# Sums of weight blocks moved to GpSimd with new orders on every engine, and zero products round TensorE's first products

## The reference, cut to what matters

```python
gate = lora_add(einsum('bnh,fh->bnf', x, W_gate), x, A_gate, B_gate)   # F = 1376, H = 512
up   = lora_add(einsum('bnh,fh->bnf', x, W_up), x, A_up, B_up)
act  = silu(gate) * up
down = lora_add(einsum('bnf,hf->bnh', act, W_down), act, A_down, B_down)
# lora_add(base, inp, A, B) = base + 0.5 * (inp @ A[idx].T) @ B[idx].T
x = x + down
x = x + einsum('bct,bcd->bdt', x, weights[condition])
```

## Time and profile before

| | |
|---|---|
| median of 3 runs | 457.99 us (457.64 to 458.76) |
| the profiled execution | 457.48 us |
| its span | 455.6 us |
| TensorE busy | 437.4 us (96%), 2465 matmuls |
| VectorE busy | 335.0 us (74%), 621 instructions |
| ScalarE busy | 213.3 us (47%), 396 |
| GpSimd busy | 168.2 us (37%), 156 |

### The profile page before, as it was taken

How to read it: one execution, slowest core, us unless ns; L and a number is a source line. 1 busy time by engine, 2 the same in 40 slices (tenths; PEclk the granted TensorE clock), 3 DMA queues, 4 the chain that set the end, 5 groups by cost and what they waited for, 6 DMA issues and landing times.

```text
span 455.6 us, 7248 instructions
## 1 busy us (share of the span) xinstructions
PE 437.4 (96%) x2465; PEld 393.9 (86%) x2465; DVE 335.0 (74%) x621; ACT 213.3 (47%) x396; POOL 168.2 (37%) x156
## 2 busy tenths in 40 slices
PE   5999999977999999999999999988999999999997
PEld 4978988865898888888888888988999999999996
DVE  6778698876876866967867857976766676676665
ACT  6664334365436335444444444925434545433441
POOL 3612120120311211111111551675566676665630
PEclk9999999999899999999999999999999999999999
DMA  8965663325667467466475589787556666555631
GB/s 268 378 221 150 182 181 108 104 81 147 167 170 210 109 163 193 112 199 157 112 205 148 141 260 337 196 201 201 170 173 192 205 199 202 176 175 175 201 104 46
DMA packets 99699, 81.12 MB, mean 178 GB/s; under 512 B 50928, under 2 KB 83056, under 8 KB 99664
## 3 DMA queue, kind: packets, MB, share of 16 engines
q1 hardware_dynamic: 88368, 47.27, 37.1%
q0 software_dynamic: 11008, 33.30, 24.0%
q10 hardware_dynamic: 288, 0.10, 0.1%
HBM read 65.18 MB, written 15.47 MB: 177 GB/s over the span
## 4 chain that ended last, share of the span: by engine, by line
PE 86%; DVE 7%; DMA 2%; ACT 2%; issue 1%; SPq 1%; DVEq 0%; ACTq 0%
PE bank L1300 24%; PE bank L1146 9%; PE bank L1147 9%; PE bank L1148 8%; PE bank L1191 8%; PE bank L1192 8%; PE bank L1193 8%; PE bank L1214 4%; PE bank L1213 4%; PE bank L1330 2%; DVE wd L763 2%; DMA actT_raw<-actT_dram 2%; PE bank L1310 1%; DVE b_gu L767 1%; PE bank L1315 1%
## 5 line engine op out<-in xcount | busy, mean ns | idle before, releaser
L441 POOL DMA_INDIRECT b_raw<-in_b_rows,rows x48 | 50.8, 1059 | 199.3 <-DVE b_gu L767 198.7
L1300 PE MATMUL bank<-wd,actT_hi 128*128 128x288 f32 x648 | 112.0, 295 | 3.1 <-DVE actT_lo L763 1.9
L1300 PEld LDWEIGHTS bank<-wd,actT_hi 128*128 128x128 f32 x648 | 95.5, 188 | 4.7 <-issue 3.5
L441 POOL DMA_INDIRECT a_dn_raw<-in_a_dn_rows,rows x64 | 75.5, 1180 | 19.5 <-issue 19.5
L767 DVE SCALAR_TENSOR_TENSOR b_gu<-b_raw,low_rows,b_gu 128x1024 fp32r<-128x1024 f32 (+1 forms) x48 | 55.6, 1159 | 30.6 <-ACT b_gu L500 30.6
L1300 PE MATMUL bank<-wd,actT_lo 128*128 128x288 f32 (+1 forms) x324 | 69.4, 296 | 0.0
L1300 PEld LDWEIGHTS bank<-wd,actT_lo 128*128 128x128 f32 (+1 forms) x324 | 51.9, 188 | 0.0
L500 ACT ACTIVATE b_gu<-b_raw 128x1024 fp32r<-128x1024 f32 (+1 forms) x48 | 46.2, 963 | 12.2 <-DMA b_raw<-in_b_rows,rows 10.7
L585 ACT ACTIVATE act<-bank 128x512 f32<-128x512 f32 (+1 forms) x48 | 26.2, 547 | 44.1 <-PE bank L1214 43.9
L763 DVE TENSOR_TENSOR actT_lo<-actT_raw,actT_hi 128x1280 fp32r<-128x1280 f32 (+1 forms) x32 | 27.0, 885 | 15.5 <-ACT actT_hi L500 14.6
L872 DVE TENSOR_TENSOR act<-act,bank 128x512 f32<-128x512 f32 (+1 forms) x48 | 29.9, 622 | 8.1 <-PE bank L1214 7.3
(11 more groups left out here) (177 smaller groups left out, 993.8 us busy)
## 6 DMA issues: line engine op xcount, KB each, us to landing
actT_raw<-actT_dram SPq DMA_DIRECT2D x16, 640.0 KB
actT_dram<-staging SPq DMA_DIRECT2D x64, 128.0 KB, 2.8
x_sb<-in_x SPq DMA_DIRECT2D x16, 256.0 KB, 2.9
xT_raw<-in_xT SPq DMA_DIRECT2D x15, 256.0 KB, 3.0
out<-out_sb SPq DMA_DIRECT2D x15, 256.0 KB, 2.0
a_raw<-in_a_gu_rows SPq DMA_DIRECT2D x56, 64.0 KB, 2.4
actT_dram<-staging SPq DMA_DIRECT2D x32, 88.0 KB, 3.1
wd_raw<-in_w_down SPq DMA_DIRECT2D x10, 256.0 KB, 7.1
```

Source lines behind the costliest of these rows:

```text
L441: return pool.indirect_dma_start(dst, None, src, bass.IndirectOffsetOnAxis(ap=rows[:, tile, col:col + 1], axis=0))
L1300: last = pe.matmul(ps_down[e][half][:, 0:HALF], a[e][0:n, c, :], wd[0:n, c, part, at:at + HALF], start=(c == 0 and i == 0), stop=(c == NC ...
```

## The change

The eight sum operations go from VectorE's queue to GpSimd's, where they stand between the gathers of pair 1. The forms are split in the order t2, t1, t4, t3, the first six of the eight parts in pair 1, t3 in pair 2. TensorE multiplies zeros (a 128x128 block by itself, into an unused bank) 34 times before its first product and 8 times after the first slice of it, as soon as VectorE has zeroed `mix_hi` and `mix_lo`. In the fast pairs the waits for the adapter halves move behind the first product of their pair of matrices. In the last pair five, not four, wd chunks are split early and at other places; the last two gatings go behind the preparation of tile 1, whose down products no longer wait for them, and the load of tile 2 goes ahead of the last spill.

The diff, cut to its core; lines with # say where a piece stands, and indentation is taken off:

```diff
+ZEROS_FIRST, ZEROS_BETWEEN = 34, 8
-SPLITS = [(f, m) for f in ("t2", "t3", "t1", "t4") for m in MATRICES]
+SPLITS = [(f, m) for f in ("t2", "t1", "t4", "t3") for m in MATRICES]
# SP, after the last pair
 load_x(0, 0)
+load_actT(2, 0)
 load_x(1, 1)
 spill(PAIRS - 1, 2)
-load_actT(2, 0)
 load_actT(3, 1)
# GpSimd: pair 1 is pair_with_sums(1); the other pairs are as before
+def sum_weights(f, i):
+    if f == "t3":
+        pool.wait_ge(w_ready, GU_PIECES)
+    elif f != "t1":
+        pool.wait_ge(weights_summed, 4 if f == "t2" else 6)
...
+    nc.gpsimd.tensor_tensor(block_raw(f, m), block_raw(a, m), block_raw(b, m), ALU.subtract)\
+        .then_inc(weights_summed, 1)
+def pair_with_sums(pr):
+    gather_b(pr, 1, 0)
+    gather_b(pr, 1, 1)
+    sum_weights("t3", 0)
+    sum_weights("t3", 1)
+    sum_weights("t1", 0)
+    sum_weights("t1", 1)
+    gather_b(pr, 2, 0)
+    sum_weights("t2", 0)
+    sum_weights("t2", 1)
+    gather_b(pr, 2, 1)
+    sum_weights("t4", 0)
+    sum_weights("t4", 1)
+    gather_b(pr + 1, 0, 0)
+    gather_b(pr + 1, 0, 1)
# ScalarE: split_forms, split_s
-    elif f == "t1":
-        sc.wait_ge(w_ready, GU_PIECES + i)
-        sc.wait_ge(weights_summed, 8)
     elif f == "t3":
         sc.wait_ge(xT_used[1], PLAIN)
-    else:
+    elif m == "up":
+        sc.wait_ge(w_ready, GU_PIECES + i - (1 if f == "t1" else 0))
+        sc.wait_ge(weights_summed, 8)
+    elif f == "t4":
         sc.wait_ge(w_ready, GU_PIECES + i)
...
-        sc.wait_ge(w_ready, GU_PIECES + 4)
+        sc.wait_ge(w_ready, GU_PIECES + 8)
# ScalarE: plain_pair
-split_forms(0, 2)
 silu(pr, 2)
 split_b(pr, 2, 0)
+split_forms(0, 2)
 split_x(pr + 1, 0)
 silu(pr, 3)
 split_b(pr, 2, 1)
+split_forms(2, 3)
 split_x(pr + 1, 1)
+split_forms(3, 6)
# ScalarE: fast_pair
-    split_forms(2, 4)
 copy_p1(pr)
 split_b(pr, 1, 0)
 silu(pr, 1)
 if first:
+    split_forms(6, 8)
     split_s(pr)
-    split_forms(4, 6)
     silu(pr, 2)
+    split_b(pr, 1, 1)
     copy_p7(pr)
-    split_forms(6, 8)
-    split_b(pr, 1, 1)
...
 if not last:
     split_x(pr + 1, 0)
+else:
+    split_down(0, 3)
...
-    split_down(0, 4)
+    split_down(3, 5)
# VectorE: plain_pair
-sum_weights("t3")
 gating(pr, 0)
 split_b(pr, 1, 0)
-sum_weights("t1")
 gating(pr, 1)
 split_b(pr, 1, 1)
-sum_weights("t2")
 split_a(pr + 1, 0)
 split_a(pr + 1, 1)
-split_forms(0, 2)
 gating(pr, 2)
 split_b(pr, 2, 0)
+split_forms(0, 2)
 split_x(pr + 1, 0)
 gating(pr, 3)
-sum_weights("t4")
 split_b(pr, 2, 1)
+split_forms(2, 3)
 split_x(pr + 1, 1)
 sum_x(pr + 1)
+split_forms(3, 6)
# VectorE: fast_pair
 split_b(pr, 0, 1)
-if first:
-    split_forms(2, 4)
 split_b(pr, 1, 0)
 if first:
+    split_forms(6, 8)
     split_s(pr)
 gating(pr, 1)
-if first:
-    split_forms(4, 6)
-else:
-    split_b(pr, 1, 1)
+split_b(pr, 1, 1)
 gate(pr, 2)
+if last:
+    split_down(0, 1)
 add_u3(pr, 0)
...
+    split_down(1, 2)
 add_u7(pr, 0)
+if last:
+    split_down(2, 3)
 add_u7(pr, 1)
# ScalarE, after the pairs
-split_down(4, NC)
-silu(PAIRS - 1, 4)
+split_down(5, NC)
 split_a_dn(1, 1)
-silu(PAIRS - 1, 5)
 sc.wait_ge(s_used, FAST)
 split_actT(1, 1)
+silu(PAIRS - 1, 4)
+silu(PAIRS - 1, 5)
...
+split_h(0, 0)
 split_a_dn(2, 0)
-split_h(0, 0)
# VectorE, after the pairs
-split_down(4, NC)
+split_down(5, NC)
+split_a_dn(1, 1)
+split_actT(1, 1)
+split_b_dn(0, 0)
+mask_td(0, 0)
 gating(PAIRS - 1, 4)
-split_a_dn(1, 1)
 gating(PAIRS - 1, 5)
-split_actT(1, 1)
...
# TensorE
+def zeros(count):
+    for _ in range(count):
+        pe.matmul(banks[7][:, 0:P], mix_hi[:, :], mix_lo[:, :], start=True, stop=True)
 def products(out_, s, t, m, cols, first, stops, wait=None, by_slice=False):
     for k in range(KH):
+        if by_slice and k == 1:
+            zeros(ZEROS_BETWEEN)
...
-        pe.wait_ge(w_ready, GU_PIECES + 3 + i)
+        pe.wait_ge(w_ready, GU_PIECES + 7 + i)
...
-    pe.wait_ge(b_ready[0], NS * pr + 2)
     for i, m in enumerate(MATRICES):
         pe.wait_ge(p1_copied, fast(pr, i))
         p2 = product(ps[m][0][:, :], xT_hi[0], xT_lo[0], 1, "b21", m, False)
         if i:
             p2.then_inc(xT_used[0], 1)
+        else:
+            pe.wait_ge(b_ready[0], NS * pr + 2)
         lora_half(ps[m][0][:, :], 0, i, PIECE)
...
+pe.wait_ge(mask_zeroed, 2)
+zeros(ZEROS_FIRST)
 base(0, 0, ramp=True, bare=True)
...
-def down(m, e, first=False):
+def down(m, e, early=False):
...
-down(0, 0, first=True)
-pe.wait_ge(act_ready, NU * PAIRS)
-down(1, 1)
+down(0, 0, early=True)
+pe.wait_ge(act_ready, NU * (PAIRS - 1) + 4)
+down(1, 1, early=True)
```

More of the change, by code:

```diff
@@ L482, in _ @@
             gather_b(0, 0, 1)
-            for pr in range(PAIRS):
+            pair(0)
+            pair_with_sums(1)
+            for pr in range(PLAIN, PAIRS):
                 pair(pr)
@@ L1078, in residual_out, with down @@
                 nc.vector.tensor_tensor(out_sb[e][:, :], x_sb[e][:, :], ps_mix[:, 0:H], ALU.add).then_inc(out_ready, 1)
-            def down(m, e, first=False, last=False):
-                if not first:
-                    mask_td(m - 1, 1 - e)
-                    split_mix(m - 1, 1 - e)
+            def down(m, e, last=False):
+                mask_td(m - 1, 1 - e)
+                split_mix(m - 1, 1 - e)
                 if not last:
                     split_a_dn(m + 1, 1 - e)
-                if not first:
-                    residual_h(m - 1, 1 - e)
+                residual_h(m - 1, 1 - e)
                 if not last:
@@ L1268, in fast_pair @@
                         p3.then_inc(s_used, 1)
+                    else:
+                        pe.wait_ge(b_ready[0], NS * pr + 3)
                     lora_half(ps[m][3][:, :], 0, i, PIECE)
```

68 lines of the change are left out of this document (29 added, 39 removed).

## The result

The changed kernel takes 468.71 us (median of 4 runs, 467.20 to 469.54), the kernel before 458.13 beside it (4 runs): ratio 1.0226, 95% interval 1.0192 to 1.0260. That is 10.6 us slower. The prediction had the sign, and a time outside its range (463.5, 456.5 to 467.0). The profiled execution has a span of 467.7 us against 455.6.

What follows compares the result with a forecast made beforehand. TensorE, busy most of the span, was taken as the bound, its idle time and clock the possible gain. 0 + 3.2 + 4.9 + 0.7 - 3.0 = +5.8 us on 457.48 gave 463.3, by the median 463.8; stated 463.5, range 456.5 to 467.

Steps and rivals of the forecast that it cites:

- the middle's orders: Pair 2 to pair 3: forms ahead of `gating(1, 4)` and later waits make TensorE late; +3.2 us.
- GpSimd's sums, with clock: Pair 1: GpSimd's sums and VectorE's two-operand work hold each other up, +4.9 us, plus +0.7 for TensorE's fallen clock.
- zeros: Start: zero products delay the first real products, but the clock is up sooner and makes up for it; 0 us.
- the end: Start of the down projection: TensorE's waits of 1.91 and 1.20 us go, tile 2 starts at 308.5; -3.0 us.
- the clock should be up after some 3.4 us of work: Start: as in pair 2, zeros raise TensorE's clock, and real products then run at twice the speed; taken as 0 us.
- the cap of 0.1 us on the gain: Start: TensorE's adapter products at 26.00 follow VectorE's queue and the gathers, so zeros can win at most 0.1 us.
- Rival (c): Start: zeros don't raise the clock; +4.9 us at most on top of either, 463 to 468 us; chance 0.12.
- `act` of (2, 3) behind late adapter rows: Start of pair 3: its gate is queued behind the last adapter load, so pair 3 starts at 125.0, +2.0 us.
- rival a: Pair 1: GpSimd's sums run beside VectorE and cost it nothing; 458.2 to 458.9 us, no change; chance 0.28.
- If sums and these take turns: Pair 1: sums and VectorE's 12.9 us of two-operand work alternate, both through at 89.4 instead of 84.5; +4.9 us.

Runs made afterwards that it cites:

- after_nozeros_vsums: The changed kernel without its zero products and with the eight weight sums back on VectorE at their old places; 460.93 us, ratio 1.0052.
- after_nozeros: The changed kernel without its 42 zero products; 469.48 us, ratio 1.0228.
- zeros_wide: The kernel before with 9 and 1 zero products of 512 columns at the start, in place of 34 and 8 of 128; 459.11 us, ratio 1.0013.
- vsums_late_again: Second profile of after_nozeros_vsums with its last three form parts moved behind the second b split of pair 2; 459.09 us, one run.
- zeros_only: The kernel before with the change's 34 and 8 zero products, nothing else; 461.37 us, ratio 1.0071.

## Why the prediction was wrong, step by step

The traces of before, after_nozeros_vsums, after_nozeros and the changed kernel add one part after another, and give each term of the sum a size where it acts: how much later the down projection begins, and what the stretch behind that takes. They are one execution each, 12.1 us apart in all, where the medians are 10.6 apart.

| term | predicted | in the traces |
|---|---|---|
| the middle's orders | +3.2 | +5.5 (289.30 to 294.85) |
| GpSimd's sums, with clock | +5.6 | +6.0 (294.85 to 300.85) |
| zeros | 0 | +3.1 (300.85 to 303.92) |
| the end | -3.0 | -2.5 (166.30 to 163.78) |

- *Zeros, 0 us.* Wrong, and the largest miss: +3.1 here, +3.2 by themselves. The step that failed is "the clock should be up after some 3.4 us of work": it took the work of pair 2, wide products, as the measure for products of 128 columns that take 0.22 us each, and the clock was still low when they ended at 8.7. Their duration (0.22) was right, and the cap of 0.1 us on the gain fits zeros_wide, where a clock raised at 7.58 won nothing. Rival (c) (up to +4.9) held. That the medians with and without zeros agree in the changed kernel would be luck for the 0: after_nozeros begins the down projection 3.1 us sooner and loses 3.0 again to the stall there and the clock behind it, which stood in no term.
- *The middle's orders, +3.2.* The first steps held: VectorE's forms in turn with ScalarE ahead of `gating(1, 4)`, TensorE idle 3.5 (3.85 in after_nozeros_vsums), a row of 2.6 before p7 (2.35). What failed is the clock behind these waits: 0.50 for 4.9 us after the first, 0.58 for 3.6 after the second. The prediction priced neither in this term and let TensorE run from p7 to pair 3 in 15.7 us, at full speed. It takes 17.16 (110.42 to 127.58), and that, not `act` of (2, 3) behind late adapter rows, is what holds pair 3: the gate is done at 126.74, 0.8 us before TensorE comes. The two paths are close (16.8 was predicted for the rows), and in vsums_late_again TensorE does wait 1.50 us for `act`. Pair 3 starts 4.6 us later than before (0.5 of it from the start), not 2.0, and a wait of 0.55 for the b split (136.34) and what follows it add 0.9.
- *GpSimd's sums, 4.9 and 0.7 of clock.* Duration (2.4, measured 2.38) and mechanism were right, and side by side (rival a) fell. The step that failed is the account "If sums and these take turns": they did not take turns one by one. VectorE was held 8.98, 4.84 and 3.52 us (the three long instructions less their usual durations), 17.3 in all, and got rid of 9.4 us of sums: 7.9 net. `sum_x` ends at 92.43 in after_nozeros and at 85.29 in after_nozeros_vsums, 7.1 us later and not 4.9. By p7 6.2 of it are left (116.61 and 110.42), so the term as a whole is off by only 0.4: its parts err in opposite ways. The prediction's own row could have shown the long hold: the gather at 291.54 in the earlier trace rows ends 0.82 us after the last of seven back-to-back low parts, held over the whole run and not over one of them. Nothing of VectorE's own work ran inside GpSimd's runs of sums but the few operations without two SBUF operands; work behind the held one, for which TensorE waited (3.01 us in pair 1), was late too. The Trainium skill ("SBUF — State Buffer", Who interferes with whom) has the second instruction block fully, whichever issues first holding the ports for the whole instruction. The fills without reads, which hold nothing up, agree with its restriction to instructions that read SBUF. The full block agrees too, but not its length: by that rule VectorE would get in after one sum of 2.38 us, and the 9.40 us span four. The measurement decides.
- *The end, -3.0.* The waits went as predicted and tile 2 followed without one. Measured -2.5 in the changed kernel, +0.8 alone (within its interval), -2.1 with the mix products at chunk 7. The size was wrong for two reasons. Both waits were taken from one execution: 1.91 stands in all six profiles with the old end (1.89 to 2.07), but 1.20, TensorE waiting for tile 2's low part behind a load that landed late, is 0.36 at most in the other five, as here in zeros_only. By these about 2 us were to be had, not 3. And TensorE, no longer stopped by those waits, met in ten of twelve profiles without the zeros a stall without a releaser, and in three the slow clock behind it, which no term had.

```profile
315.41 0.77 PE L1308 MATMUL bank<-wd,actT_hi 128*128 128x288 f32 x4 [0.36 <-issue]
```

By medians the steps are +2.7 for the orders with the end, +8.5 for the sums and -0.8 for the zeros. They must add up to the 10.5 between the medians and prove nothing more. The sums' 8.5 against the 6.0 of the table is, as far as these traces show, the stall and the low clock behind it, which the run without sums on GpSimd met less of.

## What to carry to other kernels

Before work goes from VectorE to GpSimd, look at what both read: sums of two SBUF operands on GpSimd held VectorE for 17.3 us, where making them there cost it 9.4, and only fills without reads lay beside. A chain in front of the instruction that TensorE waits for costs what reaches beyond TensorE's arrival and the slow clock after the wait (some 3 us in the medians for a chain of 5.7 here), so place it behind, and look for a split that fits into an existing wait (4.2 us here, together with TensorE's waits moved behind a product). Of products that are to raise TensorE's clock, try the form by itself (34 narrow ones, with 8 more, cost 3.2 us and raised nothing), and read first which wait comes next: here it would have taken back any gain. And before a wait is priced, see whether it stands in a second profile: 1.20 us at the down projection did not.

## What the runs showed that was not expected

- 34 products of 128 columns (0.22 us each) left the clock low until 13.7 to 15.2 us (10.1 to 14.1 without them); 9 of 512 columns brought it up by 7.6; values of 0 or 0.37 made no difference.
- Behind the same wait of 2.31 us the clock fell in some executions and not in others, and cost 1.6 us where it fell.
- VectorE's instruction with two SBUF operands stayed blocked over four GpSimd sums in a row (9.40 us), not over one.
- TensorE stood still for 0.4 to 2.4 us without a releaser near the start of the down projection in ten of twelve profiles, in pieces whose place differs between executions of one kernel, and not at all in the two profiles that had the zeros.
- At the start the granted clock in the records reads 1.00 while products of 352 columns last 0.49 us; only their durations show the lower level there.
